# Sharing the expert blocks between two token halves: 39 blocks in place of 46 in the first expert phase

## The reference

```
x = x + 0.5 * ffn(layernorm(x))
x = x + attention(layernorm(x))          # causal, one head of 128
x = x + 0.5 * ffn(layernorm(x))          # the same weights again
ffn: probs = softmax(x @ router_w.T)     # 8 experts
     the best two of them, weights renormalised
     sum over the two: weight * (gelu(x @ w1[e]) @ w2[e])     # 128 -> 512 -> 128
```

## Time and profile before

| | before |
|---|---|
| device time, median of 3 runs | 318.69 us (318.63 to 318.81) |
| span of the profiled execution, first to last instruction | 315.9 us |
| PE busy | 246.4 us (78%) |
| DVE / ACT / POOL busy | 140.2 / 143.4 / 167.0 us |

### The profile page before, as it was taken

The page is one execution under the profiler, slowest core; times in us unless marked ns, Lnnn a source line. Parts: engine busy times, 40 slices in busy tenths (PEclk is TensorE's granted clock), DMA queues, the critical chain, the costliest instruction groups (busy, mean ns, idle before and its releaser), DMA issues.

```text
span 315.9 us, 6013 instructions
## 1 busy us (share of the span) xinstructions
PE 246.4 (78%) x1985; PEld 229.9 (73%) x1985; DVE 140.2 (44%) x538; ACT 143.4 (45%) x279; POOL 167.0 (53%) x196
## 2 busy tenths in 40 slices
PE   1603999999999969899498880889995999999700
PEld 0503899999999959567276560889994999999700
DVE  4589257422113334758984664454110111343305
ACT  3332765555556631446322550746554365564300
POOL 4705777374457760277171774013777775555740
PEclk9999999999999997899857797799999799999965
DMA  7980423322246751212000111411114422422115
GB/s 203 341 213 25 118 78 51 61 87 76 83 157 197 145 197 35 66 53 57 18 0 0 44 51 52 118 42 52 50 55 116 125 83 82 157 67 72 48 68 173
DMA packets 31613, 29.37 MB, mean 93 GB/s; under 512 B 3608, under 2 KB 26016, under 8 KB 31584
## 3 DMA queue, kind: packets, MB, share of 16 engines
q1 hardware_dynamic: 25552, 18.21, 19.0%
q0 software_dynamic: 4992, 10.25, 12.4%
q10 hardware_dynamic: 1040, 0.52, 0.6%
HBM read 15.69 MB, written 13.28 MB: 92 GB/s over the span
## 4 chain that ended last, share of the span: by engine, by line
PE 56%; DVE 13%; POOL 12%; DMA 9%; issue 7%; ACT 1%; POOLq 0%; SPq 0%; DVEq 0%; ACTq 0%
PE bank L1099 21%; PE bank L1111 21%; POOL slots_in L468 5%; POOL y_rows L480 3%; PE bank L1087 3%; DVE xs L896 3%; PE bank L1151 2%; POOL xb_first L457 2%; PE bank L1050 2%; PE bank L1034 2%; PE bank L1154 2%; DMA xb_pack<-slots_in 2%; DMA y_rows<-slots_out,slot_of 1%; DMA slots_in<-xn_numbered,slot_of 1%; DMA router_rows<-in_L_ffn_router_w 1%
## 5 line engine op out<-in xcount | busy, mean ns | idle before, releaser
L1099 PE MATMUL bank<-xT_pack,w_block 128*128 128x128 f32 x736 | 100.5, 282 | 5.7 <-DVE xT_pack L850 5.7
L1111 PE MATMUL bank<-w_sb,act 128*128 x736 | 98.1, 279 | 0.2 <-issue 0.2
L1099 PEld LDWEIGHTS bank<-xT_pack,w_block 128*128 128x128 f32 x736 | 92.4, 198 | 6.6 <-DVE xT_pack L850 6.6
L1111 PEld LDWEIGHTS bank<-w_sb,act 128*128 128x128 f32 x736 | 90.5, 195 | 0.8 <-issue 0.7
L566 ACT ACTIVATE act<-bank 128x512 f32<-128x512 f32 x92 | 54.9, 597 | 77.9 <-PE bank L1099 77.8
L560 ACT COPY w_block<-w_sb 128x512 f32 x92 | 56.0, 613 | 16.6 <-issue 8.9
L457 POOL DMA_INDIRECT xb_first<-xn_rows,row_in x46 | 44.8, 974 | 34.2 <-DVE row_in L819 15.9
L480 POOL DMA_INDIRECT y_rows<-slots_out,slot_of x32 | 30.4, 951 | 26.8 <-DMA slots_out<-yb_pack 17.7
L468 POOL DMA_INDIRECT slots_in<-xn_numbered,slot_of x32 | 30.8, 961 | 16.9 <-issue 8.8
L850 DVE COPY xT_pack<-bank 128x512 f32<-128x512 f32 (+2 forms) x28 | 16.6, 594 | 51.2 <-PE bank L1087 51.1
L494 POOL DMA_INDIRECT final_rows<-xb_first,row_of x23 | 22.0, 958 | 28.7 <-DVE xb_first L869 22.3
(11 more groups left out here) (123 smaller groups left out, 253.6 us busy)
## 6 DMA issues: line engine op xcount, KB each, us to landing
w_sb<-in_L_ffn_w SPq DMA_DIRECT2D x8, 512.0 KB, 7.8
xb_pack<-slots_in SPq DMA_DIRECT2D x10, 258.0 KB, 2.9
slots_out<-yb_pack SPq DMA_DIRECT2D x10, 256.0 KB, 2.7
slots_in<-numbered SPq DMA_DIRECT2D x6, 387.0 KB, 4.8
y_rows<-final_rows SPq DMA_DIRECT2D x8, 256.0 KB, 4.1
xs<-in_L_attn_x SPq DMA_DIRECT2D x4, 256.0 KB, 4.0
out<-xs SPq DMA_DIRECT2D x8, 128.0 KB, 1.8
xb_first<-xn_rows,row_in POOLq DMA_INDIRECT x46, 2.9
```

The lines of the kernel that those rows point to most:

```text
L1099: mm = nc.tensor.matmul(h_of(c)[:, q * P:(q + 1) * P], w1_block[c % WIDE_BUFS][:, q * P:(q + 1) * P], xT_pack[n % 2][:, j * P:(j + 1) * P] ...
L1111: mm = nc.tensor.matmul(y_ps[n % 2][:, j * D:(j + 1) * D], act[c % WIDE_BUFS][:, q * P:(q + 1) * P], w2_sb[:, bass.ds(at + q * D, D)], sta ...
```

## The change

The first expert phase no longer keeps the two groups' blocks apart. Group 0 fills whole blocks for each expert first (between `SURE_BLOCKS` = 9 and 16 of them), the rows that are over go into one block per expert that is shared with group 1, and group 1's rows beyond that into further blocks. At most `SHARED_BLOCKS` = 39 blocks are needed, and 39 are computed. Only the first 9 are known from group 0's routing alone, so:

- DVE finishes both groups' routing (`route_first`, `route_second`) before it copies the first block's turned rows. Group 1's layernorm for the router is made like group 0's: ACT centres the tiles, PE transposes them (all ahead of the blocks), POOL normalises the rows for the gather (`normalise_rows(1)`) instead of DVE.
- The block's place of a row takes more steps (`place_first`, `leave_for_second`, `place_second`); the experts of the last 30 blocks are found from 24 segments rather than 8.
- Packs: 1,2,3,3 | 1,2,3,4,4 | 4,4,4,2,2. The first four are group 0's sure blocks; after nine all of group 0's rows are computed.
- POOL gathers all 39 blocks, the last 30 of them only once both routings are known, then runs `gather(0)` and `gather(1)` without interleaving.
- The combines of group 0 stand at s = 33, 36, 39, the fourth one behind the phase. rstd and normalisation are done for tiles 0 to 3 beside blocks (`FIRST_NORMS`) and for tiles 4 to 7 behind the fourth combine.
- ACT makes both groups' exponentials ahead of the first gelu. V and the attention's probabilities take the buffers `act` in place of their own, `xb_first` grows to 39 blocks. `ranks` in the code below is the PSUM view of the ranks, `over_tiles` a broadcast.

```diff
+SHARED_BLOCKS = (TILES * P * TOP + (P - 1) * E) // P
+SURE_BLOCKS = -(-(GT * P * TOP - (P - 1) * E) // P)
+LATER_BLOCKS = SHARED_BLOCKS - SURE_BLOCKS
+BLOCKS = (SHARED_BLOCKS, GROUPS * MAX_BLOCKS)
+PHASE_STARTS = (0, SHARED_BLOCKS, sum(BLOCKS))
...
+SHARED_PACKS = [1, 2, 3, 3] + [1, 2, 3, 4, 4] + [4, 4, 4, 2, 2]
+APART_PACKS = [1, 2] + [PACK] * 10 + [2, 1]
...
+SURE_PACKS, FIRST_DONE_PACKS = 4, 9
...
-        FIRST_TRANSPOSES_BESIDE = 0, 1
-        COPIES_BESIDE = 0, 1
-        FIRST_LOGITS_BESIDE = 4
-        FIRST_RANKS_BESIDE = 9
-        FIRST_ROWS_BESIDE = 15
         FIRST_FILL = 6
         TURN_W_BESIDE, QK_W_BESIDE = 19, 21
-        FIRST_PIECES = (0, 1, 5, 6, 7, 10, 11, 12, 13, 14, 15, 16)
-        FIRST_COMBINES = (36, 39, 42, 45)
-        FIRST_NORM = 46
-        RSTD_OF_ROWS = {0: 1, 2: 4}
-        FIRST_RETURN = 11
-        FIRST_RETURN_WAITS = (29, 33, 37, 41)
-        FETCHED_AMID = ((11,), (12, 13), (), ())
+        FIRST_PIECES = (3, 5, 7, 9)
+        FIRST_COMBINES = (33, 36, 39)
+        FIRST_NORMS = (37, 38, 39, 40)
+        RSTD_OF_ROWS = {0: 1, 1: 2, 2: 5}
...
-            for n in range(m * PACKS, (m + 1) * PACKS):
-                yield n, min(1, len(blocks_of(n)) - 1)
+            for n in packs_of_phase(m):
+                yield n, len(blocks_of(n)) - 1 if n == SURE_PACKS - 1 else min(1, len(blocks_of(n)) - 1)
...
-                if n in (0, GROUP_PACKS):
-                    pool.wait_ge(xn_stored[g], 16)
-                    pool.wait_ge(rows_known, g + 1)
-                if n > 2:
-                    pool.wait_ge(xT_ready, n - 1)
+                if n == 0:
+                    pool.wait_ge(xn_stored[0], 16)
+                    pool.wait_ge(rows_known, 1)
+                if n == SURE_PACKS:
+                    pool.wait_ge(xn_stored[1], 16)
+                    pool.wait_ge(rows_known, 3)
...
             normalise_rows(0)
-            for n in range(FIRST_RETURN):
+            normalise_rows(1)
+            for n in range(PACKS):
                 gather_in(n)
-            returning = gather(0)
-            for i in range(GT // 2):
-                pool.wait_ge(h_ready, FIRST_RETURN_WAITS[i])
-                some_of(returning, TOP * GT // 4)
-                for n in FETCHED_AMID[i]:
-                    gather_in(n)
-            for _ in chain(returning, gather(1)):
-                pass
+            gather(0)
+            gather(1)
             normalise_rows(2)
...
+            for r in range(GROUPS):
+                for h in range(2):
+                    centre(r, h)
+                    copy_nT(NORM_OF_ROUTE[r], h)
...
+            sc.wait_ge(logits_ready, 2)
+            nc.scalar.copy(raw_logit[:], early_logit_ps).then_inc(raw_copied, 1)
+
             exp_logits(1)
+            expert_phase(0, lambda s: None)
...
+            def place_first():
+
+                dve.wait_ge(ranked, 1)
+                last = seg_end[:, 0:E]
+                then(v.tensor_tensor(over[:], count_ps.unsqueeze(2).to_broadcast([P, E, GT]),
+                                     block_end[:], ALU.is_ge))
+                then(v.tensor_reduce(n_full[:], over[:], AX, ALU.add))
+                v.tensor_scalar(full_rows[:], n_full[:], float(P), None, ALU.mult)
+                v.scalar_tensor_tensor(spare[:], n_full[:], -float(P), count_ps, ALU.mult, ALU.add)
+                then(v.tensor_tensor_scan(last, n_full[:], n_full[:], 0.0, ALU.add, ALU.bypass))
+                v.scalar_tensor_tensor(shift[:], e_no[:], last[:, E - 1:E], last, ALU.add, ALU.subtract)
+                then(v.tensor_tensor(first_block[:], last, n_full[:], ALU.subtract))
+                v.tensor_tensor(beyond[:], ranks, over_tiles(full_rows[:]), ALU.is_ge)
+                then(v.scalar_tensor_tensor(slot[:], over_tiles(first_block[:]), float(P), ranks, ALU.mult, ALU.add))
+                then(v.tensor_tensor(beyond[:], beyond[:], over_tiles(shift[:]), ALU.mult))
+                then(v.scalar_tensor_tensor(slot[:], beyond[:], float(P), slot[:], ALU.mult, ALU.add))
+                yield
+
+            def leave_for_second():
+
+                then(v.tensor_scalar(shared_step[:], e_no[:], seg_end[:, E - 1:E], None, ALU.add))
+                v.tensor_scalar(room[:], spare[:], -1.0, float(P), ALU.mult, ALU.add)
+                v.tensor_scalar(seg_end[:, E:2 * E], shared_step[:], 1.0, None, ALU.add)
+                then(v.scalar_tensor_tensor(shared_base[:], shared_step[:], float(P), spare[:], ALU.mult, ALU.add))
+
+            def place_second():
+
+                dve.wait_ge(ranked, 2)
+                then(v.tensor_tensor(n_rest[:], count_ps, spare[:], ALU.add))
+                then(v.tensor_tensor(over[:], n_rest[:].unsqueeze(2).to_broadcast([P, E, GT]),
+                                     block_end[:], ALU.is_gt))
+                then(v.tensor_reduce(more[:], over[:], AX, ALU.add))
+                then(v.tensor_tensor_scan(last_more[:], more[:], more[:], 0.0, ALU.add, ALU.bypass))
+                v.tensor_scalar(seg_end[:, 2 * E:3 * E], last_more[:], seg_end[:, E - 1:E], float(E), ALU.add, ALU.add)
+                then(v.tensor_tensor(first_block[:], last_more[:], more[:], ALU.subtract))
+                then(v.scalar_tensor_tensor(shift[:], first_block[:], -1.0, rev_e[:], ALU.add, ALU.add))
+                yield
+                v.tensor_tensor(beyond[:], ranks, over_tiles(room[:]), ALU.is_ge)
+                then(v.tensor_tensor(slot[:], ranks, over_tiles(shared_base[:]), ALU.add))
+                then(v.tensor_tensor(beyond[:], beyond[:], over_tiles(shift[:]), ALU.mult))
+                then(v.scalar_tensor_tensor(slot[:], beyond[:], float(P), slot[:], ALU.mult, ALU.add))
+                yield
...
+            def route_first():
+                yield from pick(0)
+                yield from place_first()
+                slots_of_picks(0)
+                yield
+                yield from one_hot(0)
+                experts_of(0, SURE_BLOCKS, seg_end[:, 0:E], 0)
+                leave_for_second()
+                yield
+                dve.wait_ge(rows_written, 1)
+                v.tensor_copy(row_in[:, 0:SURE_BLOCKS], row_ps[:, 0:SURE_BLOCKS]).then_inc(rows_known, 1)
+                then(v.tensor_copy(row_so_far[:], row_ps[:, 0:MAX_BLOCKS]))
+                yield
+
+            def route_second():
+                yield from pick(1)
+                yield from place_second()
+                slots_of_picks(1)
+                yield
+                yield from one_hot(1)
+                dve.wait_ge(rows_written, 2)
+                both = MAX_BLOCKS - SURE_BLOCKS
+                v.tensor_tensor(row_in[:, SURE_BLOCKS:MAX_BLOCKS], row_ps[:, 0:both],
+                                row_so_far[:, SURE_BLOCKS:MAX_BLOCKS], ALU.add).then_inc(rows_known, 1)
+                v.tensor_copy(row_in[:, MAX_BLOCKS:SHARED_BLOCKS], row_ps[:, both:LATER_BLOCKS]).then_inc(rows_known, 1)
+                yield
+                wide = [1, LATER_BLOCKS, SEGMENTS - 1]
+                then(v.tensor_tensor(past_seg[:], any_block_no[0:1, SURE_BLOCKS:SHARED_BLOCKS].unsqueeze(2).to_broadcast(wide),
+                                     seg_end[0:1, 0:SEGMENTS - 1].unsqueeze(1).to_broadcast(wide), ALU.is_ge))
+                then(v.tensor_reduce(expert_f[:], past_seg[:], AX, ALU.add))
+                then(v.tensor_copy(seg_no[:], expert_f[:]))
+                then(v.tensor_scalar(seg_no[:], seg_no[:], E - 1, None, ALU.bitwise_and))
+                v.tensor_scalar(expert_at[:, SURE_BLOCKS:SHARED_BLOCKS], seg_no[:], H, None, ALU.mult).then_inc(routed, 1)
+                dve.wait_ge(routed, 2)
+                yield
...
+            second_rstd = rstd_of(GT, GT)
+            next(second_rstd)
+            next(second_rstd)
+            dve.wait_ge(consts, 16)
+            first_route, second_route = route_first(), route_second()
+            for _ in range(3):
+                next(first_route)
+            rest(second_rstd)
+            rest(first_route)
+            rest(second_route)
+            pieces = chain(gates(0), gates(1))
+            norm_pieces = chain(rstd_of(0, HALF), normalise_half(NORM_OF_ATTEND[0], 0))
...
             rest(pieces)
             rest(norm_pieces)
-            rest(gates(1))
+            combine_and_count(0, pair_of(3))
+            rest(rstd_of(HALF, HALF))
+            rest(normalise_half(NORM_OF_ATTEND[0], 1))
...
             logits(0)
-            pe.wait_ge(consts, 13)
+            transpose_both(NORM_OF_ROUTE[1])
+            pe.wait_ge(consts, 16)
             ranks(0)
+            logits(1)
             rows(0)
+            ranks(1)
+            rows(1)
```

361 lines of the change are left out of this document (185 added, 176 removed).

## The result

The changed kernel takes 319.28 us (317.59 to 321.15, 20 runs), the kernel before on the same chip 318.42 (313.98 to 319.34, 20 runs): ratio 1.0072 [1.0044, 1.0101], that is 2.3 us. (The ratio leaves out runs over 1.5% above the fastest of their kernel, which here are six of the kernel before and none of the changed one; between the medians lie 0.9 us, between the means of all runs 1.8.) Predicted were 315.1 us and a gain of 3.6.

A forecast was written before the change was run, and what follows sets the result against it. PE was taken to bound the expert phases, 1.90 us a block; 11.8 - 18.2 + 2.7 = -3.7, taken as 3.6 off 318.69, gave 315.1 us, with 312.7 to 318.2 for 8 in 10.

The forecast's parts named there:

- Term 1: Opening: both groups' routing ahead of the first block moves its first product to 43.2 us, +11.8.
- Rival 4: Opening: DVE and POOL exclude each other, up to 5.7 us more than taken, 320.8 us; chance 0.07.
- Term 2: First expert phase, first product to last second product: 79.45 us in place of 97.7, -18.2.
- The way to block 3: Phase start: from the first product to block 3's first product 7.1 us, 7.93 before.
- the slow clock: Phase start: PE's longer rest keeps the second and third products slow; none to 1.7 us, 0.7 taken.
- The stall of 0.7: Phase end: PE waits for the last pack's turned rows behind gathered results; none to 3 us, 0.7 taken.
- rival 3: Phase end: gathered rows land late and the old stall returns, up to 319.5 us; chance 0.17.
- Term 3: Behind the phase: PE's end to Q takes 5.9 us, 3.2 before, +2.7; exp's table load costs nothing.
- From Q on, both versions run the same program: From Q's first product to the end: distance unchanged at 183.7 us.
- rival 5: Rewritten opening: something not foreseen, to either side; chance 0.11.
- rival 2: Opening without contention, clock rising as early as before, no stall: 313.2 us; chance 0.15.

The follow-up runs named there:

- both: Changed kernel plus eight extra PE products at the first blocks and PE's and ACT's offset loads regrouped: 314.60 us, ratio 0.9919 to the kernel before.
- warm: Changed kernel plus eight extra unread PE products, six behind ranks(1), two behind the first pack's turn: 316.34 us, ratio 0.9981 to the kernel before.
- again: Changed kernel run once more without any edit: 319.66 us, ratio 1.0081 to the kernel before.
- align: Changed kernel with PE's and ACT's offset loads regrouped to start at 9, 13, 16, then every fourth block: 318.36 us, ratio 1.0043 to the kernel before.
- before_again: Kernel before, run once more unchanged: 318.94 us, ratio 1.0006.
- fill_q4: Changed kernel plus four extra PE products between the transposes of Q's two halves: 318.29 us, ratio 1.0056 to the kernel before.

## Why the prediction was wrong

**Term 1, the opening: right.** +11.74 where +11.8 was said, first product 43.12 for 43.2; `row_in` at 26.99 for 27.15. Some of this agreement is luck of the draw: in the two repeats the kernel before had its first product at 30.38 and 30.42, since its router's rows had landed by 5.0 and 4.9 us and not by 6.3; the changed kernel's stood at 43.1 to 43.4 each time, so against them the opening costs 12.8. Rival 4 did not occur. With both engines at work it was POOL that paid:

```profile
8.61 6.23 POOL L471 TENSOR_SCALAR xn_numbered<-xs,moments,rstd 128x128 f32<-128x128 f32 x8 [3.83 <-DVE rstd L735]
17.86 8.46 POOL L471 TENSOR_SCALAR xn_numbered<-xs,moments,rstd 128x128 f32<-128x128 f32 x8 [3.02 <-DVE rstd L735]
```

The second normalisation lay beside DVE's placing and took 8.46 us in place of 6.23; DVE's 64-column operations beside it kept their 0.21 to 0.23, all but one of 0.36. By the rule of the Trainium skill that rival 4 took (SBUF — State Buffer, Who interferes with whom), where the one that issued first holds up the other for its whole instruction, DVE would have waited as well; in this trace the 0.14 us of that one operation are the longest wait of such an operation that could be its.

**Term 2, the phase: its blocks right, two of its sizes wrong.** -15.4 where -18.2 was said. The blocks behind the first three came out (71.3 us in `both`, 70.95 in the sum). The way to block 3 was taken too long, 7.1 us without the slow clock where `warm` and `both` have 5.9. The stall of 0.7 did not come: gathers started at 102.37 (predicted 100.2), the copy of the last pack's turned rows came at 117.79 (said: 116.3) with PE in work from 117.17 to 119.85, so nothing waited and rival 3 did not occur. The step that failed here is "so that the slow clock ... may last into the second and third product; none to 1.7, I take 0.7": it lasted through four products in the profile after, through two and a part of the third in `again`, and cost 3.6 and 2.5 us of the way to block 3 (9.5 and 8.4 against the 5.9 of `warm`), 3.3 in the medians. I had bounded it from one row of the kernel before; the change makes PE rest longer ahead of block 0. The second is a term that was missing, the offset loads: 1.3 by `align`. They stand in the very queue that sets the phase, and the new packs and the new count changed both their place in the pack and their length.

**Term 3, the tail: +3.1 where +2.7 was said**, 0.44 too small. PE's last transposes took 0.88 to Q, at the low clock, where 0.3 was taken.

**"From Q on, both versions run the same program": this step failed too.** From Q to the end of the span were 183.7 and became 187.1. The prediction itself called this what would make its frame wrong, and it did. Between these two profiles all of it is phase 2, +4.1; Q to phase 2 is 0.5 shorter, for Q and V ran at the low clock in both. Of the 4.1 us 1.3 are the kernel before's own luck (`before_again`), 0.8 the changed kernel's (`again`), and some 2 are left, about 1.0 at the first blocks and 1.0 where the second group's begin. The second goes with offset loads of 1.0 us in place of 0.33, so the program is not quite the same either; the prediction had no term for them in either phase. The first stays open: filling the pause ahead of phase 2 brought the first block to the high clock and no time, since DVE's copy then ends the wait, and what sets the clock at the blocks behind it was not found. Q's low clock is a cost against the fast executions of the kernel before only. PE rests 4.28 us ahead of Q's second half, and filling that took 1.0 to 1.4 us off (`fill_q4`). The projection of group 1 took 3.63 and 3.78 us in the two profiles after and 3.78, 2.62 and 2.64 in the three before, where 1.96 is the high clock; filling its pause was not tried.

In the spans the prediction had 312.3 us and the profile after has 318.8, 6.5 more: -0.1 in the opening, +2.8 in the phase, +0.4 in the tail, +3.4 from Q on. The phase's 2.8 are 2.9 for the clock (3.6 - 0.7), -1.2 for the way to block 3 without it, 1.4 for the loads, 0.4 for the other blocks and -0.7 for the stall. In the medians the miss is 4.2 us (319.28 for 315.1); the profiled execution took 1.4 more than the median. So what happened was the unforeseen case, rival 5, with 0.11, and not one of the mechanisms named; rival 2, that the opening is cheaper, was the opposite of the case.

## What to carry to other kernels

Work taken out of a PE-bound phase is worth its time only if PE is as warm as before at each stage's start: ask for every pause that a change makes longer which products follow it, and price them at the low clock, near twice their length. A serial chain ahead of the first block costs its full length, here 11.7 us of the 15 that the shared phase gives; cut it and run it beside the blocks that don't need it, which gave 7.7 back here. Where an index is counted anew, look at the small loads that go by it, in the stages too that were to stay the same. A single profile of a kernel whose runs spread over 2% is one draw: take a second before a stage of it is called unchanged.

## What was not expected of the hardware

- A 128x128 by 512-column f32 product takes two records of 0.44 us, 0.87 us in all, at the high clock.
- TensorE's clock was at its low level (1.2 GHz, a block's product 2.07 us for 1.06 at 2.4) for up to four products behind an idle TensorE, also where small work lay between. At Q 4.28 us idle were followed by the low level (3.62 us), 0.84 by the high (1.96), and 1.33 in the kernel before by either (3.44 once, 1.96 twice). The profile's granted clock read 1.00 in the stretch of 43 to 51 us where the products took 2.07, so the level there is inferred from their length.
- A register load of four offsets takes 0.33 to 0.55 us in PE's queue when it begins at an element of `expert_at` whose number is divisible by four, 1.00 to 2.55 otherwise, in every load of the 18 profiles. Three of 1.9 to 2.1 us in the changed kernel delayed the products behind them by 0.33 to 0.46.
- The table load of the softmax took 1.28 us at 135.97, in time where ACT waited 1.55 more for DVE: it cost nothing, as term 3 had it.
